# A four-block sequence model on one core: a new order of slots in the attention steps, and two edits of the feed-forward part

## The reference, cut to what matters

```
x = ln(x + mamba(x))            # L0_attn: conv, selective scan, gate
x = ln(x + fp4_ffn(x))          # L0_ffn: blockwise quantised gate/up/down
x = ln(x + diff_attention(x))   # L1_attn
x = ln(x + sign_mlp(x))         # L1_ffn
```

```
scale = max(max|xb| / 6, 1e-12);  xn = xb / scale
q = GRID[searchsorted(MID, |xn|)] * sign(xn) * scale     # FP4 grid
h = silu(q(x) @ q(w_gate).T) * (q(x) @ q(w_up).T);  out = q(h) @ q(w_down).T
```

```
q, k = rope(x @ Wq.T), rope(x @ Wk.T);  v = x @ Wv.T
w1, w2 = softmax(q1 k1 * 8**-0.25), softmax(q2 k2 * 8**-0.25)
o = w1 @ v - lam * (w2 @ v)
o = (o * rsqrt(mean(o**2) + eps) * ln_w + ln_b) * (1 - LAMBDA_INIT);  out = o @ Wo.T
```

## Time and profile before

| what | us |
|---|---|
| median of 3 runs | 1046.54 |
| lowest and highest run | 1043.47, 1051.39 |
| the profiled execution, its own time | 1046.28 |
| its span, first to last instruction | 1044.5 |
| mean granted TensorE clock over the span | 0.962 |

### The profile page before, as it was taken

One profiled execution on the slowest core, in us unless ns is written; L12 is line 12 of the kernel. 1 busy time (PEld: TensorE's weight loads), 2 busy tenths in 40 slices (PEclk: granted clock), 3 DMA queues, 4 the chain that ended last, 5 costly groups with the idle time before them and its releaser, 6 DMA issues.

```text
span 1044.5 us, 14399 instructions
## 1 busy us (share of the span) xinstructions
PE 897.4 (86%) x4356; PEld 460.3 (44%) x4356; DVE 887.4 (85%) x1337; ACT 718.4 (69%) x1585; POOL 795.1 (76%) x576
## 2 busy tenths in 40 slices
PE   7798989798989797786886779899989888799995
PEld 2333434343434342234554554555555443355544
DVE  4799999999999999998885677878787874489996
ACT  3685959595959596554555466777777778687861
POOL 2798999999999999875776854576767536677762
PEclk9899999999999999899998899999999999899997
DMA  5852535343344434003301343324342300000001
GB/s 152 324 237 88 205 120 204 121 182 143 156 169 169 157 152 174 0 1 80 65 0 31 91 109 85 99 82 115 81 111 78 107 3 3 0 2 21 10 21 31
DMA packets 35167, 103.89 MB, mean 99 GB/s; under 512 B 3659, under 2 KB 22475, under 8 KB 24395
## 3 DMA queue, kind: packets, MB, share of 16 engines
q1 hardware_dynamic: 35095, 103.03, 29.3%
HBM read 93.71 MB, written 8.91 MB: 98 GB/s over the span
## 4 chain that ended last, share of the span: by engine, by line
DVE 29%; PE 24%; ACT 19%; issue 19%; POOL 5%; DMA 3%; SPq 1%; DVEq 1%; POOLq 0%; ACTq 0%
PE bank L1655 12%; DVE bank L333 7%; PE bank L2012 5%; ACT bank L461 4%; DVE m_hC L342 4%; DVE a_nm L1417 4%; PE bank L611 3%; ACT L461 2%; DVE m_hS L333 2%; ACT late L1590 1%; DMA qs<-a_nmT 1%; DVE bank L916 1%; DVE m_du L347 1%; DVE x_all L122 1%; PE bank L1181 1%
## 5 line engine op out<-in xcount | busy, mean ns | idle before, releaser
L559 POOL TENSOR_TENSOR m_dBu<-m_du,m_Bt 128x1024 f32<-128x1024 f32 x128 | 299.6, 2358 | 14.0 <-DMA m_Bt<-bcd 11.6
L611 PE MATMUL bank<-m_hC,ident 128*128 128x512 f32 x512 | 256.6, 626 | 52.2 <-POOL m_hC L569 24.1
L333 DVE TENSOR_TENSOR_SCAN bank<-bank,m_dBu 128x512 f32<-128x512 f32 x184 | 220.8, 1215 | 5.4 <-POOL m_dBu L559 4.1
L1417 DVE TENSOR_REDUCE a_nm<-bank 128x2 f32<-128x512 f32 x256 | 169.3, 686 | 56.2 <-PE bank L1655 55.8
L1590 ACT ACTIVATE late<-bank 128x512 f32<-128x512 f32 x256 | 146.5, 603 | 61.0 <-PE bank L1655 59.8
L611 PEld LDWEIGHTS bank<-m_hC,ident 128*128 128x128 f32 x512 | 93.6, 196 | 195.3 <-issue 92.5
L461 ACT ACTIVATE bank<-m_delta,early 128x510 f32<-128x510 f32 x256 | 169.8, 676 | 0.3
L342 DVE TENSOR_TENSOR m_hC<-bank,m_Ct 128x512 f32<-128x512 f32 x184 | 122.5, 666 | 0.0
L1655 PE MATMUL bank<-ks,qs 72*128 72x256 bf16 x512 | 98.8, 276 | 18.8 <-DVE a_nm L1417 18.6
L1655 PE MATMUL bank<-qs,ks 99*128 99x256 bf16 x512 | 98.6, 275 | 9.7 <-ACT late L1590 4.6
L458 ACT ACTIVATE bank<-m_zero 128x2 f32<-128x2 f32 x181 | 30.5, 169 | 111.0 <-DVE m_hC L342 110.5
(11 more groups left out here) (219 smaller groups left out, 1744.1 us busy)
## 6 DMA issues: line engine op xcount, KB each, us to landing
m_Bt<-bcd SPq DMA_DIRECT2D x32, 1024.0 KB, 7.0
m_Ct<-bcd SPq DMA_DIRECT2D x32, 1024.0 KB, 6.6
qs<-parts SPq DMA_DIRECT2D x16, 576.0 KB
ks<-parts SPq DMA_DIRECT2D x48, 192.0 KB
parts<-a_part SPq DMA_DIRECT2D x32, 192.0 KB, 3.0
out<-x_all SPq DMA_DIRECT2D x8, 256.0 KB, 2.3
vx<-in_vrow SPq DMA_DIRECT2D x4, 256.0 KB
qs<-in_fill SPq DMA_DIRECT2D x1, 768.0 KB
```

The costliest lines, as they stand in the source:

```text
L333: nc.vector.tensor_tensor_scan(out, decay, dBu[:, g % RD], 0.0, ALU.mult, ALU.add).then_inc(scan_ready, 1)
L559: nc.gpsimd.tensor_tensor(dBu[:, g % RD:g % RD + CH], du[:, n % 2], Bt[:, s].unsqueeze(1).broadcast_to([P, CH, GTOK]), ALU.mult).then_inc( ...
L611: return nc.tensor.matmul(out, lhsT, rhs, start=start, stop=stop)
L1417: nc.vector.tensor_reduce(nm[:, slot % 2, q, 2 * pair:2 * pair + 2], s1[i % 2][:], AX.X, ALU.max, negate=True).then_inc(max_ready, 1)
```

## The change

1. `f.LONE` goes from 6 to 5 and the empty attention step -5 is no longer called: attention step -5 now stands beside feed-forward step 5, and single gate banks begin with group 5.
2. Tile 3 of the feed-forward step moves from mark 5 to mark 3, behind tile 2, on PE, ACT and DVE.
3. `magic_x` takes its multiplier 2^22 + 2 from a PSUM bank (`magic_one`, set once), broadcast, in a scalar_tensor_tensor instead of a tensor_scalar with two immediates.
4. x's transpose, `xT` (now two buffers), the q/k product, `qk` and `rotate` run for batch n+5 instead of n+4. The split into parts stays at batch n+4 but starts at unit 0 of the step: ACT unit 12 to 0, POOL 9 to 1, ACT 15 to 3, POOL 11 to 5.
5. `split_max` leaves DVE (units 3 and 4) for POOL (unit 3), the same five operations.
6. Other units: V's product stays at 0, its copy 3 to 5; second `weighted` pair 1, 2 to 3, 4; `copy_sums` of it 3 to 5, `turn_sums` 5 to 7, `leave` 6 to 8, `difference` 7 to 9, square 9 to 10, `mean_square` 11 to 12, `head_norm` 14 to 13; q/k product 4 to 5; transposes of the maxima 7 to 6 and their copy 8 to 7; `normalize` 8 to 6, `add_bias` 4 to 7, `rotate` 7 to 9.
7. The banks of V and of the way in are exchanged in the steady state (V in `ma`, x and q/k in `mb`), and the waits go with them. The wait for `q_in` moves from POOL's `residual_middle` to SP, ahead of the parts' DMA.

```diff
-    f.LONE = 6
+    f.LONE = 5
...
         def magic_x(m):
             dve.wait_ge(x_abs, m)
-            nc.vector.tensor_scalar(qx.magic[:], qx.magic[:], 1.0, 2.0 ** 22 + 2.0, ALU.max,
-                                    ALU.mult).then_inc(x_magic, 1)
+            dve.wait_ge(one_ready, 1)
+            nc.vector.scalar_tensor_tensor(out=qx.magic[:], in0=qx.magic[:], scalar=1.0,
+                                           in1=magic_one.unsqueeze(2).broadcast_to([P, NXB, QB]),
+                                           op0=ALU.max, op1=ALU.mult).then_inc(x_magic, 1)
...
             hidden(n, 2)
+            hidden(n, 3)
             if has(n + 2):
                 magic_x(n + 2)
             yield
-            hidden(n, 3)
             yield
...
             gate_up(n, 2)
+            gate_up(n, 3)
             residual(n - 2)
...
-        def split_max(m, slot, step):
+        def split_max(m, slot):
+            b = 5 * m
+            src = nm[:, slot % 2]
+            pool.wait_ge(max_ready, MAPS * m + MAPS)
+            wait(pool, nm_turned, m)
+            nc.gpsimd.tensor_copy(nmp[:, :, 0], src).then_inc(nm_chain, 1)
+            pool.wait_ge(nm_chain, b + 1)
+            nc.gpsimd.tensor_tensor(nmr[:, 0], src, nmp[:, :, 0], ALU.subtract).then_inc(nm_chain, 1)
...
-            wait(pool, o_ready, min_group(m - 4, BATCH))
+            wait(pool, o_ready, min_group(m - 5, BATCH))
...
+                if u == 1 and has(n, 4):
+                    residual_high(n + 4)
+                if u == 0 and has(n, -3) and not has(n, 4):
+                    normalize(n - 3)
+                if u == 3 and has(n, 1):
+                    split_max(n + 1, slot + 1)
+                if u == 5 and has(n, 4):
+                    residual_middle(n + 4)
+                if u == 6 and has(n, -3) and has(n, 4):
+                    normalize(n - 3)
+                if u == 7 and has(n, 0):
                     add_bias(n)
+                if u == (10 if lone(n) else 9) and has(n, 5):
+                    rotate(n + 5)
+                if u == 13 and has(n, -1):
                     head_norm(n - 1)
...
+                if u == (1 if n < -1 else 0) and has(n, 4):
+                    m = n + 4
+                    act.wait_ge(rope, 2 * m + 2)
+                    nc.scalar.activation(part[:, 0], rot[:], ACT.Copy).then_inc(split_a, 1)
...
-            alone(attention(-5, -5 % ATT_RING))
```

More of the change, by code:

```diff
@@ L1085, in step @@
             silu(n, 2)
+            silu(n, 3)
             yield
@@ L1094, in step @@
             yield
-            silu(n, 3)
             yield
@@ L1365, in body @@
                 sp.wait_ge(split_p, 2 * m + 2)
+                wait(sp, q_in, 64 * m)
                 for i in range(2):
@@ L1615, in body @@
                     nc.scalar.activation(bias[:], ma[:, 0:P], ACT.Copy).then_inc(bias_copied, 1)
-                if u == 8 and has(n, 1):
+                if u == 7 and has(n, 1):
                     m = n + 1
@@ L1624, in body @@
                     nc.scalar.activation(oT[:], turned_heads(n), ACT.Copy).then_inc(oT_ready, 1)
-                if u == 9 and has(n, -1):
+                if u == 10 and has(n, -1):
                     m = n - 1
@@ L1631, in body @@
                     copy_sums(n, 0)
-                if u == 12 and has(n, 4):
-                    m = n + 4
-                    act.wait_ge(rope, 2 * m + 2)
-                    wait(act, parts_out, 32 * m)
-                    wait(act, split_p, 2 * m)
-                    nc.scalar.activation(part[:, 0], rot[:], ACT.Copy).then_inc(split_a, 1)
                 if u == 15 and has(n, -2):
                     squares(n - 2)
-                if u == 15 and has(n, 4):
-                    act.wait_ge(split_p, 2 * (n + 4) + 1)
-                    nc.scalar.activation(part[:, 1].rearrange("p a t -> p (a t)"), res[:], ACT.Copy).then_inc(split_a, 1)
                 yield
@@ L1711, in body @@
                     m = n + 3
-                    wait(pe, qk_ready, m + 1)
-                    wait(pe, oT_ready, min_group(n - 2, BATCH))
-                    for t in range(TS):
-                        last = mm(mb[:, P * t:P * t + P], xT[:, P * t:P * t + P], wqkv[:, 2 * P:3 * P])
-                    last.then_inc(v_done, 1)
-                if u in (1, 2) and has(n, -1):
-                    weighted(n - 1, (slot - 1) % RING, 1, u - 1)
-                if u == (3 if lone(n) else 1) and has(n, 4):
-                    m = n + 4
-                    pe.wait_ge(f.norm_chain, m // 2 + 1)
@@ L1729, in body @@
                     wait(pe, r_ready, n - 2)
                     for t in range(TS):
-                        last = nc.tensor.transpose((mb if lone(n) else ma)[:, P * t:P * t + P],
-                                                   k.x_all[:, TS * m + t, :], ident)
+                        last = mm((mb if lone(n) else ma)[:, P * t:P * t + P], xT[:, m % 2, P * t:P * t + P],
+                                  wqkv[:, 2 * P:3 * P])
+                    last.then_inc(v_done, 1)
+                if u == (3 if lone(n) else 1) and has(n, 5):
+                    m = n + 5
+                    pe.wait_ge(f.norm_chain, m // 2 + 1)
+                    wait(pe, qk_ready, m)
+                    if lone(n):
+                        wait(pe, v_ready, n + 4)
+                    wait(pe, oT_ready, n - 2)
+                    for t in range(TS):
+                        last = nc.tensor.transpose(mb[:, P * t:P * t + P], k.x_all[:, TS * m + t, :], ident)
@@ L1733, in body @@
                     last.then_inc(x_turned, 1)
-                if u == (6 if lone(n) else 4) and has(n, 4):
-                    m = n + 4
+                if u in (3, 4) and has(n, -1):
+                    weighted(n - 1, (slot - 1) % RING, 1, u - 3)
+                if u == (6 if lone(n) else 5) and has(n, 5):
+                    m = n + 5
                     pe.wait_ge(xT_ready, m + 1)
-                    if lone(n):
-                        wait(pe, v_ready, m)
                     for z in range(2):
-                        last = mm((mb if lone(n) else ma)[:, SEQ * z:SEQ * z + SEQ], wqkv[:, P * z:P * z + P], xT[:])
+                        last = mm(mb[:, SEQ * z:SEQ * z + SEQ], wqkv[:, P * z:P * z + P], xT[:, m % 2])
```

93 lines of the change are left out of this document (40 added, 53 removed).

## The result

| | us |
|---|---|
| before, median of 6 runs (lowest, highest) | 1046.55 (1043.47, 1051.39) |
| after, median of 6 runs (lowest, highest) | 1022.66 (1021.10, 1023.66) |
| ratio, 95% interval | 0.9769 (0.9742 to 0.9796) |
| the profiled execution after: own time, span | 1023.18, 1021.4 |

Faster, by 23.9 us; the forecast was 1020.2, so the total came 2.5 us from it. The profiled executions differ by 1046.28 - 1023.18 = 23.1 us, and the table shares those out. A stretch runs from the start of one instruction to that of another (`scale_h` of a group, exp of unit 0 of a step).

A forecast was written before the change was run, and what follows sets the result against it. No engine bounds it all; in attention PE has no slack and waits for DVE's row maxima. Attention 16.5, feed-forward 5.1 and handover 4.5 make 26.1 us, from 1046.28 to 1020.2, its own range 1011 to 1031, overall 1006 to 1040.

The forecast's parts named there:

- Edit 2, 5.1 us: Feed-forward steps 2 to 5: tile 3 sooner removes DVE's idle pieces before it, 1.73 + 3 x 1.12 = 5.1 us.
- Edit 3, zero net: Feed-forward `magic_x`: constant from a bank costs 0 to 0.26 us in seven steps, offset by covered waiting; zero net.
- Edits 1 and 4, 4.5 us: Handover, groups 5 to 7: ACT's 4.87 us rope wait goes; 35.35 us becomes 30.9, gain 4.5, bounds nothing and 8.
- POOL sets the two steps: Feed-forward steps 6 and 7 beside attention: POOL's work, 14.2 us a step, sets their length.
- another wait of ACT for POOL, now at unit 1: Handover's lower bound: such a wait in front of h's abs costs as much as the old one, gaining nothing.
- The 2.5 us that I had added for `back_x`: Feed-forward step 5: rope 0 is issued ahead of x_sub of group 7, so DVE's `back_x` waits about 2.5 us.
- Edit 5: Attention's `split_max` on POOL: takes 1.4 us a step from DVE, costs POOL 1.5 us, with 1.1 us of slack.
- rivals 3 and 4: `split_max` on POOL: dear at 0.81 us an instruction, up to 1042 us (0.12); or taking over the step, 1056 (0.06).
- Edit 6, 15.8 us a step: Attention steps 3 to 10: new units end PE's waits for maxima; ACT's chain closes a step at 15.8, against 16.97.
- rival 1: Attention: ACT's chain loses its row maximum, so a step is PE's own 14.8 us; 1009 us in all, chance 0.12.
- Steps 0 to 2, 46.8 us: First attention steps: 14.3 + 15.5 + 17.0 = 46.8 us against 49.98, gain 3.2.
- Steps 11 to 13, 46.2 us: Late attention steps, with less on PE and ACT: 15.7 + 15.3 + 15.2 = 46.2 us against 50.18, gain 4.0.

The follow-up runs named there:

- e7: Kernel before with tile 3 sooner on PE, ACT and DVE and magic_x's constant from a bank; attention and handover as before: 1040.61 us, 0.9950.
- e6: Kernel before with only feed-forward tile 3 sooner, on PE, ACT and DVE; magic_x in its old form: 1053.77 us, 1.0086.
- e2: Kernel after with ACT's second part copy moved from unit 3 to 7 in the steps without scores: 1017.97 us, 0.9733.
- e3: Kernel after with ACT's first part copy behind exp of unit 1 instead of unit 0, in steps with scores: 1018.40 us, 0.9742.
- e8: Kernel after with both ACT copy moves, those of e2 and e3, together: 1016.19 us, 0.9715.
- e1: Kernel before with tile 3 sooner on DVE alone, by oversight; PE and ACT keep it at mark 5: 1053.46 us, 1.0080.
- e12: e8 with mean_square in unit 11 and ACT's q/k product copy in unit 8 instead of 7 in steps without scores: 1015.02 us, 0.9696.

## Why the prediction was right, and where it was not

- **Edit 2, 5.1 us.** The size holds, but only with edit 3 beside it. From group 1 to 4 the profile gained 4.5 us (forecast 4.0; another 0.5 came before group 1, where nothing was edited), e7's gained 6.1 from group 1 to 5 (forecast 5.1), and e7 is 5.2 us faster in all. Step 5 gave 1.8 us back (15.36 us against 13.54), now that attention step -5 stands beside it: DVE waits there 1.44 us for ACT's abs, behind the copy of the q/k product, and attention's constants on DVE (about 1.6 us), which before came after group 5, come before it.
- **Edit 3, zero net.** Wrong, and the step that failed most. I compared its 0.69 us with the 0.43 of the old form at its old place. At the new place the old form takes up to 3.38 us. Edit 3 is worth 10.1 us in after and 13.2 beside edit 2 alone, and without it edit 2 makes the kernel slower, by 0.9% (e6). I had quoted the rule of the Trainium skill on the shared ports and then looked at `difference`, not at the instruction that was moved. The sum was right because the change holds both.
- **Edits 1 and 4, 4.5 us.** Wrong: 1.9 us between groups 5 and 7 in the profile, and nothing over the middle stretch. The term "POOL sets the two steps" failed; its own lower bound ("another wait of ACT for POOL, now at unit 1") was nearly the place, one copy later: unit 3, in front of silu 2. With that copy moved (e2) the stretch is 29.02 us against the forecast 30.9. The 2.5 us that I had added for `back_x` were 1.29.
- **Edit 5.** The price was right (1.4 us against 1.5), the slack too (1.24 measured, 1.1 forecast), so rivals 3 and 4 were properly small. Its worth was not: I had put all of PE's waits down to what leaves DVE, and undoing edit 5 costs 2.3 us.
- **Edit 6, 15.8 us a step.** 15.71 measured, by the loop named: PE to unit 13, row maximum, residual, ACT's four pieces, scores of unit 3. e3 confirms the loop. Within it two sizes offset each other: PE's part ended at 10.9 us, where I had 11.8, and from there to the end of the row maximum it took 2.2 us, where I had 1.2; `mean_square` (0.41 us), which I had left out, stands there too. My PE-packed step of 14.8 (rival 1) was too low: with two pieces off the loop the step is still 15.27, and in e8 PE is busy for 121.6 of the 123.0 us of steps 3 to 10. I had taken the waits of the weight loads (2.16 us) for time in which PE stood. The products waited 1.23 us, and PE was busy for 123.9 / 8 = 15.5 us a step already before.
- **Steps 0 to 2, 46.8 us.** 46.76, by luck: 15.61, 15.37 and 15.79 us, where I had 14.3, 15.5 and 17.0.
- **Steps 11 to 13, 46.2 us.** 44.38: 15.17, 14.84 and 14.37 us against 15.7, 15.3 and 15.2. The lengths were sized too high. The end of the DMAs' stalls is not what I missed, since 15.7 is a full step without one; and in before PE's products waited for these DMAs 2.8 us in all, in three places. In the code, x's transposes and the q/k product now end with step 10, so step 11 does without them; what that is worth no run shows. Landing of the 48 DMAs of the maxima after, against the earlier trace rows:

```profile
DMA to landing us min/median/max: 1.8/1.8/3.2
```

Before it was 4.3 in the median and 6.1 at most, and in after nothing waits for them. e7 keeps attention as before, and its DMAs land as late (4.3 and 6.2), yet these three steps took 55.2 us there, against 49.6 in e1, 49.7 in e6 and 50.18 in before. The difference is step 13, which took 20.55 us instead of 15.83. Its window, where the number ahead of the last two is the granted clock:

```profile
830.93:851.48 20.55, 19.25 (x116) 8.17 (x114) 13.29 (x29) 11.18 (x25) 5.37 (x6) 0.75 0.01 2
```

PE had waited 1.39 us for the last maxima just before, until 830.50. From 831.6 on the clock was at 1.2 instead of 2.4 GHz for 3.4 us, and again for 6.8 us from 841.9 (granted 0.51 and 0.50), and PE's `weighted` pieces took 1.85 and 1.94 us instead of 1.07. In before PE waited 1.17 us at that place and the clock stayed at 1.00 through step 13. Whether the wait brought the clock down no run was made to show; if it did, a late DMA costs more there than the wait itself. Every kernel with the new order whose split was left alone took 44.4 or less. The spread of before's runs goes with the clock as well: of the 39 beside the experiments, the six under 1043.5 us had a mean clock of 0.962 to 0.968, the three over 1050 one of 0.956 to 0.959. After's runs spread over 2.6 us only, but e12's, with the same order of DMAs, over 6.6.
- **The tail, about nothing within 3 us.** 0.9 us longer.

The profiled execution missed the forecast by 3.0 us, because the errors offset: 5.6 us too much in the middle, 0.9 in the tail, and 3.6 too little in attention's steps (2.6) and ahead of group 4 (1.0).

## What to carry to other kernels

An instruction's duration belongs to its place: before moving a DVE instruction, look at what POOL runs at the new place and who starts first, and price the old form there, not where it stood. Where an in-order engine serves two parts, list for each step what waits in front of the pieces the other part needs; a copy that waits for POOL belongs behind silu, not ahead of it. To tell what a many-part plan owes to each part, undo one at a time: here two parts that were thought to pay could each be undone for nearly nothing, and one priced at zero was worth 10 us. Undo them together too, since each may stand in for the other; that was left out here. And take PE's idle time from its products, not from its weight loads, which overlap them.

## What the runs showed of the hardware that I had not expected

- A DVE tensor_scalar of 0.43 us stood 3.38 us beside a POOL tensor_tensor of 3.17 that had started 0.07 us before it; a DVE cast of 32 columns took 1.15 us beside a POOL instruction of 1.16.
- The same attention step took 15.83 us at a granted clock of 1.00 and 20.55 at 0.75 (step 13 of before and of e7).
- Ten POOL casts of 128x32 that wait for nothing start 0.15 us apart; the five of the split, each behind a semaphore, start 0.29 to 0.31 apart. The spans are 0.21 to 0.24 in both. For such small casts the wait between them is half of the price. The Trainium skill ("Perfetto Trace Analysis", GPSIMD Engine Instruction) advises to time GpSimd by the spacing of starts rather than by spans. The rows agree: ten spans of 0.21 us would be 2.1 us, and the ten took 1.51.
